# The low-weight pass of both projections at 154 columns instead of 256

## The reference

```python
Q = (img_embed @ Wq).reshape(B, -1, H, D).transpose(0, 2, 1, 3)
K = (sent_embed @ Wk).reshape(B, -1, H, D).transpose(0, 2, 1, 3)
V = (sent_embed @ Wv).reshape(B, -1, H, D).transpose(0, 2, 1, 3)
score = jnp.einsum('bhqd,bhkd->bhqk', Q, K) / math.sqrt(D)
attn = softmax(where(mask, score, -inf))
ctx = jnp.einsum('bhqk,bhkd->bqhd', attn, V).reshape(B, -1, H * D)
out = ctx @ Wo + img_embed        # then a layer norm with gamma and beta
```

## Time and profile before

| | |
|---|---|
| median of 3 runs | 378.53 us (377.85 to 378.63) |
| span of the profiled execution | 376.4 us |
| its own time outside the span | no separate figure; the runs' median is 2.1 us above the span |
| TensorE matmul busy | 363.8 us, 97% |
| VectorE busy | 297.6 us, 79% |
| ScalarE busy | 215.7 us, 57% |
| GpSimd busy | 221.9 us, 59% |

### The profile page before, as it was taken

One profiled execution on the slowest core, in us unless ns is written; L12 is line 12 of the kernel. 1 busy time (PEld: TensorE's weight loads), 2 busy tenths in 40 slices (PEclk: granted clock), 3 DMA queues, 4 the chain that ended last, 5 costly groups with the idle time before them and its releaser, 6 DMA issues.

```text
span 376.4 us, 6759 instructions
## 1 busy us (share of the span) xinstructions
PE 363.8 (97%) x2352; PEld 337.9 (90%) x2352; DVE 297.6 (79%) x483; ACT 215.7 (57%) x750; POOL 221.9 (59%) x195
## 2 busy tenths in 40 slices
PE   6999999999999999999999999999999999999991
PEld 3899999999999998899889989998998899889880
DVE  3899999988788676877787787768777877877796
ACT  4775776677766476564466446545654664465610
POOL 0564464365338112577767766776777577667555
PEclk9999999999999999999999999999999999999997
DMA  7997767975631602134143142242341440411012
GB/s 227 400 404 259 273 259 273 344 266 210 213 151 59 224 0 57 58 112 141 52 145 129 41 168 84 86 141 80 117 139 47 150 137 34 167 50 63 30 57 84
DMA packets 20642, 55.81 MB, mean 148 GB/s; under 512 B 1664, under 2 KB 4224, under 8 KB 18560
## 3 DMA queue, kind: packets, MB, share of 16 engines
q1 hardware_dynamic: 20464, 55.29, 41.3%
q10 hardware_dynamic: 144, 0.08, 0.2%
HBM read 46.98 MB, written 8.39 MB: 147 GB/s over the span
## 4 chain that ended last, share of the span: by engine, by line
PE 86%; DVE 5%; POOL 3%; ACT 2%; DMA 1%; issue 1%; SPq 1%; POOLq 0%
PE pair L373 28%; PE pair L306 26%; PE pair L399 26%; PE pair L385 4%; DVE w_out_lo L583 2%; DMA w_proj<-wk 1%; PE pair L358 1%; POOL out_sb L756 1%; ACT prob L507 1%; SPq L254 1%; POOL var_eps L745 1%; POOL w_proj_lo L761 1%; ACT w_out_hi L470 1%; POOL centred L752 1%; DVE kv_t L603 1%
## 5 line engine op out<-in xcount | busy, mean ns | idle before, releaser
L507 ACT ACTIVATE prob<-masked,neg_max 128x77 f32<-128x77 f32 x256 | 88.3, 348 | 100.3 <-DVE neg_max L639 100.3
L761 POOL TENSOR_TENSOR w_proj_lo<-w_proj,w_proj_hi 128x768 fp32r<-128x768 f32 x30 | 56.0, 1891 | 60.6 <-ACT w_proj_hi L462 60.6
L306 PE MATMUL pair<-kv_t,w_out_hi 128*128 128x308 f32 x256 | 65.1, 305 | 0.0
L399 PE MATMUL pair<-vw_hi,pt_hi 128*128 128x512 f32 (+1 forms) x160 | 63.2, 395 | 0.0
L399 PE MATMUL pair<-vw_lo,pt_hi 128*128 128x512 f32 (+1 forms) x160 | 63.1, 394 | 0.0
L399 PE MATMUL pair<-vw_hi,pt_lo 128*128 128x512 f32 (+1 forms) x160 | 62.5, 391 | 0.0
L373 PE MATMUL pair<-a_hi,xt_hi 128*128 128x308 f32 x256 | 59.4, 313 | 0.0
L745 POOL TENSOR_SCALAR var_eps<-mean_var 128x1 f32<-128x1 f32 x32 | 24.2, 757 | 58.7 <-DVE mean_var L677 58.4
L306 PE MATMUL pair<-kv_t,w_out_lo 128*128 128x256 f32 x256 | 58.5, 280 | 0.0
L373 PE MATMUL pair<-a_lo,xt_hi 128*128 128x308 f32 x256 | 57.1, 304 | 0.0
L373 PE MATMUL pair<-a_hi,xt_lo 128*128 128x308 f32 x256 | 57.0, 304 | 0.0
(11 more groups left out here) (54 smaller groups left out, 683.6 us busy)
## 6 DMA issues: line engine op xcount, KB each, us to landing
w_out<-wq_t SPq DMA_DIRECT2D x8, 1024.0 KB, 6.1
w_out<-wo SPq DMA_DIRECT2D x8, 1024.0 KB, 4.8
xt_in<-x_tiles SPq DMA_DIRECT2D x16, 512.0 KB, 3.8
x_in<-x_rows SPq DMA_DIRECT2D x16, 512.0 KB, 4.3
out<-out_sb SPq DMA_DIRECT2D x32, 256.0 KB, 2.1
w_proj<-wv SPq DMA_DIRECT2D x8, 768.0 KB, 4.6
w_proj<-wk SPq DMA_DIRECT2D x6, 768.0 KB, 7.5
w_proj<-wk SPq DMA_DIRECT2D x4, 192.0 KB, 4.6
```

The costliest lines, as they stand in the source:

```text
L306: mm = pe.matmul(pair[:, bank, 0:n], w[:, k, cols], moving[:, k, 0:n], start=(at == 0), stop=(at == len(steps) - 1))
L399: mm = pe.matmul(ps_out[:, i % 2, 0:s.model], ps[0:rows, j, :], v[0:rows, b, j, :], start=(j == 0 and n == 0), stop=(j == s.key_t - 1 and ...
L507: e = act.activation(prob[i % 2][:, cols], masked[i % 2][:, cols], ACT.Exp, bias=neg_max[i % 2][:, h:h + 1], accum_out=sums[i % 2][:, h:h ...
L761: pool.tensor_tensor(half_cols(w_proj_lo[u % W_RING], half), half_cols(w_proj_sb[u % W_RING], half), half_cols(w_proj_hi[u % 2], half).bit ...
```

## The change

The constant `FAST_COLS` goes, and the lo matmul of `short_product` takes `s.toks` = 154 columns. The 308 columns of the hi matmul, the number of matmuls, their order, their waits and all other engines' instructions stay as they are. The products of remainder with remainder are no longer computed.

```diff
-FAST_COLS = 256
...
-        assert FAST_COLS <= 2 * self.toks <= BANK and self.model <= BANK and self.dim_t == self.model_t == 4
+        assert 2 * self.toks <= BANK and self.model <= BANK and self.dim_t == self.model_t == 4
...
             def short_product(pair, bank, w_hi, w_lo, moving, m, tiles):
 
                 cols = slice(m * P, (m + 1) * P)
-                steps = [(w, n, k) for k in range(tiles) for w, n in ((w_hi, 2 * s.toks), (w_lo, FAST_COLS))]
+                steps = [(w, n, k) for k in range(tiles) for w, n in ((w_hi, 2 * s.toks), (w_lo, s.toks))]
                 steps[-2:] = steps[:-3:-1]
                 for at, (w, n, k) in enumerate(steps):
                     mm = pe.matmul(pair[:, bank, 0:n], w[:, k, cols], moving[:, k, 0:n],
```

## The result

The changed kernel takes 376.17 us, the median of 4 runs (375.72 to 376.24), against 378.58 us of the kernel before on the same chip (377.85 to 378.65): ratio 0.9938, with a 95% interval of 0.9926 to 0.995. The forecast was 448.2 us and its range 373 to 460 us; the time lies in the range, with the sign of the forecast wrong. That it lies in the range is no merit of the forecast: the range had been widened downwards to take in the floor, to which 0.12 was given. The profiled execution has a span of 373.9 us, 2.5 us under that of before.

A forecast was written before the change was run, and what follows sets the result against it. TensorE's unbroken matmul stream was taken to bound the kernel: span 376.4 + 70.8 us for dearer lo matmuls - 1.1 us of waits = 446.1, plus 2.1 us from span to run median, 448.2 us; range 373 to 460.

The forecast's parts named there:

- the floor: In TensorE's stream, a matmul with fresh weights comes no sooner than 110 ns after the one before; chance 0.12.
- the fallback: Lo matmul of 154 columns handled as full-format four passes, 276.8 ns against 118.8; +70.8 us over 448; chance 0.66.
- Rival 1: Lo matmuls fall from 118.8 to 110 ns, 3.9 us saved, VectorE's room covering it; 374.6 us, chance 0.12.
- The line: TensorE matmul cost by width, 6.4 ns + 0.439 ns a column, fitted at 308 and 512 columns; 74.0 ns at 154.
- The room of VectorE: VectorE's free time beside the matmuls: 1.95 us in the first half of the first stage, 9.7 us in the second.
- rival 2: Lo matmul at 74.0 ns saves TensorE 20.1 us, but VectorE lets through 11.7; 366.8 to some 370 us, chance 0.11.
- The distance behind a lo matmul: Start-to-start test in TensorE's timeline: 0.28 us for four passes, 0.11 floor, 0.07 line, 0.13 dearer column.
- The piece of 56 matmuls: Test in the chain of waits, 7.29 us before: 11.7 for four passes, 7.05 floor, 6.0 line, 7.7 dearer column.

The follow-up runs named there:

- bf_grp: Changed kernel with each block's lo matmuls placed together and bf16 remainders in both projection and output product; 376.18 us, ratio 0.9959.
- bfp_grp: Changed kernel with each block's lo matmuls placed together and bf16 remainders in the projection alone; 373.06 us, ratio 0.9865.
- w308: Changed kernel with lo matmuls of all 308 columns instead of 154; 387.87 us, ratio 1.0246.
- w64: Changed kernel with lo matmuls of 64 columns instead of 154; 441.65 us, ratio 1.1664.

## Why the prediction was wrong

- **The step that failed** is the choice in "The change part by part": "I take the fallback, 276.8 ns". There is none. The lo matmul of 154 columns costs 111.5 ns, and 64, 110 and 200 columns cost the same within 2 ns at the high clock. I set the row nearest in width aside, the transposes at 110 ns, with the argument that a transpose multiplies nothing; it was the right row. What bounds the lo matmul is the load of the next weights; that the transposes' 110 ns are the same fits, but no run varied the transposes. A name in the kernel's text had made an unshown regime look likely. The Trainium skill's four passes for true FP32 ("FP8 and Floating Point Precision", TensorE Precision Notes) didn't reach this case: 308 and 512 columns cost 0.439 ns for each column more, and narrower ones never more than the floor. The Trainium skill gives no number of passes there for the reduced form.
- **Rival 1, the floor, is what happened**, with 374.6 us against 376.2 measured. Its floor was 110 ns and is 111.5, and its 3.9 us came out as 3.2. The other part is waits: it assumed that VectorE would never be late, and TensorE's waits grew by 0.8 us. The estimate of 107 ns from the Trainium skill ("TensorE: Matmul & The Clock Gate", LDWEIGHTS) is 4.5 ns low by these runs at the high level; at the low level the floor was about 215 ns, which that rule doesn't give, and there the measurement decides.
- **The line** of cost by width held where it was needed: 141.7 ns foreseen for 308 columns and 141.3 measured, 74 ns for 154 columns and 72 measured when bf16 made the load short.
- **The room of VectorE** can't be read from its busy time. The 55.05 of 57.00 us gave 7.29 x 55.05/57.00 = 7.04 us as the shortest use in the first half. `bf_grp` stopped at 7.13, above it, and `bfp_grp` ran at 6.81, below it, since part of VectorE's busy time is a `w_out_lo` held up beside GpSimd. What rival 2 would have lost to VectorE is open either way.
- **A test that I named was wrong.** The distance behind a lo matmul is 0.07 us, which I had written down for the line going on. The record of a matmul begins before its weights are there. The piece of 56 matmuls, 7.05 us for the floor and 7.09 measured, was the test that worked.
- Not foreseen was the clock. The low stretch at the start ends 1 us later in the trace of the changed kernel than in that of the kernel before, which is little; 44 columns fewer cost some 4 us by it.

## What to carry to other kernels

In a stream of matmuls with fresh 128 x 128 weights each, cost the matmul as the longer of its own columns and the next one's weight load. At the high clock, f32r columns up to about 240 are then free, and cutting them gains nothing; that is where 6.4 ns + 0.439 ns a column reaches 111.5, an estimate, since nothing between 200 and 256 columns was run. Cutting far below can even cost, by the clock. A shorter load, here bf16 for the small remainders placed one behind the other, gains where narrower columns can't. Take the busy time of an engine as work only where no neighbour holds it up. Price a missing row by its nearest neighbour with the same weight load, and don't take a regime from a constant's name.

## What the runs showed of the hardware that was not expected

- With narrow lo matmuls TensorE can stay at its 1.2 GHz level for long without a gap: with 64 columns 147 us (0.50 from 8 to 155 us), but only to 11.6 us when the first uses had 154 columns.
- The floor is not a fixed time. At the low level a pair with 64 columns takes 2 x 235.8 = 472 ns; 308 columns take 0.26 us of it (w308, whose matmuls start 0.26 us apart before 13 us), which leaves some 215 ns for the lo, nearly double 111.5. The loads of w64's first eight transposes, at that level, take 0.21 us each:

```profile
153.04 1.70 PEld L357 LDWEIGHTS pair<-identity,vw_t 128*128 128x128 f32 x8
154.72 0.31 PEld L305 LDWEIGHTS pair<-kv_t,w_out_hi 128*128 128x128 f32 x1
```

- A `w_out_lo` on VectorE takes 1.21 to 1.23 us while GpSimd is idle, and up to 2.57 us in the changed kernel beside GpSimd's `w_proj_lo`.
- A bf16 copy of 924 bytes a partition, placed ahead of other tensors, made 15 matmuls of 512 columns, which don't touch it, together up to 50 ns longer (3.52 against 3.47 us); placed behind them it cost nothing.
